# Three half-precision passes in place of float32 for the value and output weights of a head

## What is computed

```
wuk = w_uk.reshape(H, DN, KVL)
q_lat = jnp.einsum('bhsd,hdr->bhsr', q_nope, wuk)
scores = jnp.einsum('bhsr,btr->bhst', q_lat, c_kv) + jnp.einsum('bhsd,btd->bhst', q_rope, k_rope[:, 0])
...
out_lat = jnp.einsum('bhst,btr->bhsr', probs, c_kv)
wuv = w_uv.reshape(H, DV, KVL)
out = jnp.einsum('bhsr,hdr->bhsd', out_lat, wuv)
out = out.transpose(0, 2, 1, 3).reshape(b, s, H * DV)
return out @ w_out
```

## Time and profile before

| | |
|---|---|
| median of 3 runs | 2105.26 us (2104.92 to 2106.75) |
| profiled execution | 2106.01 us, its span 2104.2 us, clock 0.999 |
| PE busy | 2071.2 us, 98% of the span |
| DVE, ACT, POOL busy | 1274.1, 738.0, 364.9 us |
| chain that ended last | PE 96% |
| group 0's loop and the switch quad's slot 0 | about 177 to 885 us of the span |

### The profile page before, as it was taken

One profiled execution on the slowest core, in us unless ns is written; L12 is line 12 of the kernel. 1 busy time (PEld: TensorE's weight loads), 2 busy tenths in 40 slices (PEclk: granted clock), 3 DMA queues, 4 the chain that ended last, 5 costly groups with the idle time before them and its releaser, 6 DMA issues.

```text
span 2104.2 us, 29620 instructions
## 1 busy us (share of the span) xinstructions
PE 2071.2 (98%) x10688; PEld 1732.1 (82%) x10688; DVE 1274.1 (61%) x2114; ACT 738.0 (35%) x1931; POOL 364.9 (17%) x319
## 2 busy tenths in 40 slices
PE   6999999999999999999999999999999999999999
PEld 5787888888888888888888888888888768888887
DVE  4636666766666676666666666666667772333321
ACT  3324333333333333433333333333333555232221
POOL 2012212212121222121111212112121201000000
PEclk9999999999999999999999999999999999999999
DMA  5616343535353443557434244342435381202010
GB/s 212 240 62 222 105 173 103 193 115 188 115 205 121 158 135 142 201 192 265 135 115 144 70 150 134 106 154 70 150 117 198 114 313 53 81 1 81 1 41 40
DMA packets 63017, 284.78 MB, mean 135 GB/s; under 512 B 6640, under 2 KB 7280, under 8 KB 51440
## 3 DMA queue, kind: packets, MB, share of 16 engines
q1 hardware_dynamic: 62960, 284.00, 39.2%
HBM read 172.83 MB, written 111.15 MB: 135 GB/s over the span
## 4 chain that ended last, share of the span: by engine, by line
PE 96%; DVE 1%; DMA 1%; ACT 1%; POOL 0%; issue 0%; DVEq 0%; SPq 0%; ACTq 0%; POOLq 0%
PE at_out L53 11%; PE at_out L54 11%; PE at_out L55 11%; PE at_qbank L53 6%; PE at_qbank L55 6%; PE at_qbank L54 6%; PE at_qbank L946 6%; PE at_qbank L947 6%; PE at_score L738 4%; PE at_score L736 3%; PE at_turned L745 3%; PE at_qbank L692 2%; PE at_value L55 2%; PE at_value L54 2%; PE at_value L53 2%; PE at_score L737 1%
## 5 line engine op out<-in xcount | busy, mean ns | idle before, releaser
L1511 DVE TENSOR_TENSOR at_acc<-at_out,at_acc 128x512 f32<-128x512 f32 x512 | 352.1, 688 | 95.7 <-PE at_out L55 87.4
L53 PE MATMUL at_out<-at_wvo,at_val_hi 128*128 128x512 f32 x1024 | 402.5, 393 | 0.7 <-DVE at_acc L1511 0.7
L54 PE MATMUL at_out<-at_wvo,at_val_hi 128*128 128x512 f32 x1024 | 401.7, 392 | 0.0
L55 PE MATMUL at_out<-at_wvo,at_val_lo 128*128 128x512 f32 x1024 | 400.0, 391 | 0.0
L1059 ACT ACTIVATE at_probs<-at_probs,at_row_stats 128x128 f32<-128x128 f32 x512 | 199.8, 391 | 379.6 <-DVE at_row_stats L1489 379.6
L1276 POOL TENSOR_TENSOR at_probs<-at_probs,at_row_stats 128x512 f32<-128x512 f32 x128 | 133.3, 1041 | 819.1 <-DVE at_row_stats L1494 819.1
L55 PEld LDWEIGHTS at_out<-at_wvo,at_val_lo 128*128 128x128 f32 x1024 | 192.4, 188 | 42.7
L53 PEld LDWEIGHTS at_out<-at_wvo,at_val_hi 128*128 128x128 f32 x1024 | 193.3, 189 | 35.1 <-DVE at_acc L1511 1.8
L54 PEld LDWEIGHTS at_out<-at_wvo,at_val_hi 128*128 128x128 f32 x1024 | 193.0, 188 | 31.3
L1065 ACT ACTIVATE at_pT_hi<-at_turned 128x512 fp32r<-128x512 f32 x128 | 76.4, 597 | 318.6 <-PE at_turned L745 318.6
L738 PE MATMUL at_score<-at_tok,at_qrope 128*128 128x256 f32 x512 | 170.9, 334 | 0.0
(11 more groups left out here) (183 smaller groups left out, 4162.4 us busy)
## 6 DMA issues: line engine op xcount, KB each, us to landing
wvo_d<-at_wvo SPq DMA_DIRECT2D x16, 2048.0 KB, 7.4
parts_d<-at_rope_parts SPq DMA_DIRECT2D x32, 1024.0 KB, 7.0
at_qrope<-parts_d SPq DMA_DIRECT2D x128, 256.0 KB, 5.0
at_wvo<-wvo_d SPq DMA_DIRECT2D x16, 2048.0 KB, 8.5
ab_raw<-in_w_heads SPq DMA_DIRECT2D x32, 576.0 KB, 4.7
cr_ctx<-in_context SPq DMA_DIRECT2D x16, 1024.0 KB, 7.6
wabs_d<-at_wabs SPq DMA_DIRECT2D x16, 768.0 KB, 7.5
at_wabs<-wabs_d SPq DMA_DIRECT2D x16, 768.0 KB, 5.3
```

The source lines that it names most:

```text
L53: pe.matmul(out, w_hi, x_hi, start=first, stop=False)
L54: pe.matmul(out, w_hi, x_lo, start=False, stop=False)
L55: return pe.matmul(out, w_lo, x_hi, start=False, stop=last)
L1511: dve.tensor_tensor(at, outb[n][:], at, ALU.add).then_inc(added, 1)
```

## The change

In the 29 heads of the slots `absorb_head` gives way to `absorb_half`, called twice: half 0 between `values` and `output(s, 1)`, half 1 at the end of the slot. Each half is three float32r passes over 512 columns. The preparation and the opening keep `absorb_head`. The halves are cut so:

- ACT (`cut_half`): behind its `turn` it copies the head's 128 x 128 value weights to `ab_uv_hi` and the first 128 x 512 output weights to `ab_proj_hi`; behind its `values` it copies the other 128 x 512 into the same `ab_proj_hi`, once PE is through with half 0 (`ab_mm`). ACT, not PE, now waits for the ring's load.
- POOL (`cut_half`): as its first work in the slot it takes the low halves of the value weights and of the first output weights, in place in the ring; then, behind `rope_sums` if there is one but ahead of `normalise`, that of the second.
- PE waits for POOL's low half (`w_lo_done`) before each half.
- ACT's `take_head` waits in slots 5 and 7 for the end of `output(s, 1)`, since that reads the `wvo` buffer which it writes. DVE's order is unchanged.

```diff
+            def absorb_half(m, s, n, i, use, taken):
+
+                pe.wait_ge(w_lo_done, cuts(m, s, n))
+                pe.wait_ge(q_taken, taken)
+                low = ring_low[i]
+                three_passes(pe, qbank[use % 2][:], uv_hi[:], low[:, 0:DV], proj_hi[:],
+                             low[:, DV + n * CH:DV + (n + 1) * CH], True, True).then_inc(ab_mm, 1)
...
+                part = absorbed(kind, s)
+                if part and part[0] == "B":
+                    absorb_half(m, s, 0, (AHEAD + part[3]) % 2, use[s] + 1, first + use[s])
                 output(m, s, 1)
...
-                        absorb_head(i, bank_use, first + bank_use - 1)
+                        absorb_half(m, s, 1, i, bank_use + 1, first + bank_use)
...
+            def cut_half(n, i, part):
+
+                act.wait_ge(ab_mm, part + n)
+                if n == 0:
+                    act.activation(uv_hi[:], ring[i][:, 0:DV], ACT.Copy)
+                act.activation(proj_hi[:], ring[i][:, DV + n * CH:DV + (n + 1) * CH], ACT.Copy).then_inc(w_hi_done, 1)
...
+                if part and what == "B":
+                    act.wait_ge(ring_in[i], 16 * (ITEMS // 2 * m + (AHEAD + at) // 2 + 1))
+                    cut_half(0, i, count)
                 if s + 2 < end:
                     exps(m, s + 2)
...
+                if part and what == "B":
+                    cut_half(1, i, count)
...
+                        if place(s)[0] == h // 2:
+
+                            act.wait_ge(out_ready, 4 * (STEPS * m + s + 1))
                         take_head(h, use[s] + 1, count)
...
+            def cut_half(m, s, n, i):
+
+                pool.wait_ge(w_hi_done, cuts(m, s, n))
+                low = ring_low[i]
+                if n == 0:
+                    pool.tensor_tensor(low[:, 0:DV], ring[i][:, 0:DV], as_f32(uv_hi[:]), ALU.subtract)
+                cols = slice(DV + n * CH, DV + (n + 1) * CH)
+                pool.tensor_tensor(low[:, cols], ring[i][:, cols], as_f32(proj_hi[:]), ALU.subtract).then_inc(w_lo_done, 1)
...
+                if heads:
+                    cut_half(m, s, 0, (AHEAD + part[3]) % 2)
                 if finish:
                     rope_sums(first + USE[kind][s - 1] + 3)
+                if heads:
+                    cut_half(m, s, 1, (AHEAD + part[3]) % 2)
                 if s + 2 < end:
                     normalise(m, s + 2)
```

More of the change, by code:

```diff
@@ L144, in decoder @@
         ring = [home(200928 + 4 * ITEM_B * i, f"ab_raw{i}", [P, ITEM_B]) for i in range(2)]
+        uv_hi = at(TABLES + 2048, "ab_uv_hi", [P, DV], F32R)
+        proj_hi = home(198656, "ab_proj_hi", [P, CH], F32R)
+        ring_low = [home(200928 + 4 * ITEM_B * i, f"ab_low{i}", [P, ITEM_B], F32R) for i in range(2)]
         wvo, qlat, qrope = [wvo0, wvo1], [qlat0, qlat1], [qrope0, qrope1]
@@ L297, in decoder, with cuts @@
         AHEAD, ITEMS = 5, 6
+        CUT = {0: 0, 5: 1, 6: 2, 7: 3}
+        def cuts(m, s, n):
+            return len(PIECES) + 2 * (QUAD * m + CUT[s]) + n + 1
         x_chunks = x.rearrange("(c b p) d -> c p b d", c=CHUNKS, p=P)
@@ L855, in slot @@
                     rope(ROPE_AT[s], use[s] + 1, first + use[s])
[L856 removed]
+                if part:
                     what, _, _, at = part
                     i, bank_use = (AHEAD + at) % 2, use[s] + 1
[L859 removed]
                     if what == "A":
+                        pe.wait_ge(ring_in[i], 16 * (ITEMS // 2 * m + (AHEAD + at) // 2 + 1))
                         absorb_pair(i, bank_use, first + bank_use - 1)
                     else:
[L863 removed]
+                        absorb_half(m, s, 1, i, bank_use + 1, first + bank_use)
             def cross_turn(b):
@@ L1132, in slot @@
                     turn(m, s + 1)
+                part = absorbed(kind, s)
+                if part:
+                    what, h, ahead, at = part
+                    i, count = (AHEAD + at) % 2, 2 * (AHEAD + ITEMS * m + at)
+                if part and what == "B":
+                    act.wait_ge(ring_in[i], 16 * (ITEMS // 2 * m + (AHEAD + at) // 2 + 1))
+                    cut_half(0, i, count)
                 if s + 2 < end:
@@ L1145, in slot @@
                     act.activation(wqr[:, 0], wqr_raw, ACT.Copy).then_inc(wqr_hi, 1)
-                if part := absorbed(kind, s):
-                    what, h, ahead, at = part
-                    count = 2 * (AHEAD + ITEMS * m + at)
+                if part:
                     if what == "A":
@@ L1309, in slot @@
                 finish = s - 1 in ROPE_AT and end > STEPS
+                part = absorbed(kind, s)
+                heads = part is not None and part[0] == "B"
+                if heads:
+                    cut_half(m, s, 0, (AHEAD + part[3]) % 2)
                 if finish:
                     rope_sums(first + USE[kind][s - 1] + 3)
+                if heads:
+                    cut_half(m, s, 1, (AHEAD + part[3]) % 2)
                 if s + 2 < end:
```

## The result

| | before | changed |
|---|---|---|
| median of 6 runs each, us | 2105.09 | 2095.65 |
| lowest and highest | 2104.91, 2106.75 | 2094.69, 2097.34 |
| profiled execution | 2106.01 | 2096.1 |
| its span | 2104.2 | 2093.9 |

The changed kernel takes 0.9952 of the time before, with a 95% interval of 0.9942 to 0.9962: 9.4 us less. The forecast was 9.4 less, 2095.9. The passes that the title calls half-precision are the float32r passes over high and low halves.

What follows compares the result with a forecast made beforehand. PE, busy 98% at 2.4 GHz, was taken to bound the kernel. 28 heads at 0.357 us give 10.0, less 0.6 for stalls, 9.4 us: 2095.9 for the median; range 2093.5 to 2100.3.

Steps and rivals of the forecast that it cites:

- Removed and added, 0.36 a head: On PE, two float32 matmuls of 1.72 us give way to six float32r passes of 1.36: 0.36 us gained a head.
- Half 0 finds its operands: At half 0's start, ACT's copies and POOL's low halves are ready with over 2 us to spare; free.
- Half 1's chain: In slot 5, half 0's end, ACT copy, POOL subtraction, PE: operands ready 0.26 us early; then `normalise` delays the turn's load 0.10.
- The allowance of 0.02 a head: At the next slot's `turn`, behind `normalise`: 0.02 us lost a head with every link at its upper bound, 0.6 us in all.
- 28 heads, and nothing in quad 0: Quad 0's slot 0 gains nothing, as PE waits behind ACT for the rope weights' load; 28 heads left, 10.0 us.
- The clock's 1.7 us either way: Behind quad 0's wait, a lowered clock costs about 1.7 us; taken as unchanged, 1.7 either way for the range.
- Rival 4's second half: No slow clock behind quad 0's wait: 10.0 + 1.7 us gained, 2093.6; the whole rival has chance 0.04.
- The sum: Whole kernel: 10.0 - 0.6 = 9.4 us gained, 2095.9 for the median; chance 0.60.
- rival 1: Chain through `normalise` longer than its rows by 0.1 to 0.25 us: 0.05 to 0.2 a head, 2097.3 to 2101.0; chance 0.24.
- rival 3: POOL decides: PE waits each slot for `normalise` behind a subtraction of 1.85 us, not 1.29; slower, 2109.7; chance 0.03.
- Rivals 1 to 3: Chain through `normalise` too long, in three sizes; the middle one, 0.3 to 0.5 us more, gives 2102 to 2108, chance 0.09.
- The sign that the forecast named for them: In PE's list, the `turn` waiting for `at_probs` or half 1 for low halves, 0.1 us or more each slot.

Runs made afterwards that it cites:

- the repeat on one chip: The unmodified changed kernel measured again, beside the kernel before on the same chip: 2095.32 us, 0.9950 of before.
- the repeat with two subtractions: Changed kernel plus two 28-column POOL subtractions between second low half and `normalise`, run again on another chip: 2102.07 us, 0.9983 of before; first time 2101.66.

## Why the prediction was right, step by step

- **Removed and added, 0.36 a head: right in size, with luck in its parts.** The three passes of half 0 take 0.69 us and those of half 1 0.71 (352.39 to 353.10), where the rope's spacing gave 0.68 each. Why half 1's stand 0.237 apart stays open: it is so with and without `normalise` in the chain. Six passes are thus 1.40 and leave 0.32, not 0.36; the 0.04 at the start of the next slot, which I had not seen and which comes with the placing, makes it whole. Two small misses of opposite sign; the head's sum is 0.36 by the slots. The Trainium skill, FP8 and Floating Point Precision, section TensorE Precision Notes, counts true float32 as 4 passes; if every pass cost the same, three would gain 0.43 a head, an estimate. The trace doesn't agree with that gain: 1.40 us for six passes, where two float32 matmuls took 1.72, a fifth less. It doesn't refute the count of four: a quarter of one float32 matmul is 0.215 us, and a float32r pass, with a weight load of its own, took 0.227 to 0.237. The row of the pass itself was the better basis.
- **Half 0 finds its operands: right.** They are 3.6 us early, also in slot 5.
- **Half 1's chain: right to 0.04 at each point.** Counted from half 0's start, ACT's copy begins at +0.88 (forecast 0.88), POOL's subtraction at +1.60 (1.59), its end is at +2.89 (2.88), that of `normalise` at +3.89 (3.92), the turn's load at +3.94 (3.98), the turn at +4.15 (4.11 without stall). The copy took 0.64, not 0.60: my row was a copy from a PSUM bank, this one reads SBUF, which may be the reason. The 0.04 was made up by a shorter link from ACT to POOL, 0.08 where 0.11 was assumed, and by `normalise` starting 0.03 ahead of the subtraction's end. What I had no row for, POOL to PE, was 0.05.
- **The allowance of 0.02 a head: not needed, the one term of the sum that was wrong.** The load is 0.02 behind the pass ahead, forecast 0.10, and the cover for the turn is about 0.17, where I had read 0.15 from rows of another kind of matmul. So even the upper bound of 0.17 would have cost next to nothing, and the margin is 0.15 and not 0.05. Moving `normalise` out of the chain brought nothing. I had subtracted 0.6 us for it.
- **28 heads, and nothing in quad 0: right in size, the reason half right.** That PE's wait ends by the load's landing held: the copy began at 194.06 and 194.74 in the two profiles, and PE resumed 0.68 apart. Counted from the start of slot 0, the copy begins at 16.6 to 17.7 us in the ten traces, so this moves by a microsecond from one execution to the next. The 0.74 us of the difference between the traces come from there for the most part, and not from the change.
- **The clock's 1.7 us either way: a term that was mis-sized.** It is 0. I multiplied the missing clock by PE's time, though the earlier trace rows show DVE busy 2.93 of 3.00 us in that very stretch. Rival 4's second half falls with it.
- **The sum.** 10.0 less 0.6 was forecast. The 28 heads gave 10.1 by the slots and there was no stall, so the sum should have been 10.0. The medians differ by 9.4, but their interval, 8.0 to 12.2 us (0.4 to 0.6% of 2105), holds 10.0 as well, and the repeat on one chip gave 10.8. That the forecast met the median to a tenth is luck; its mechanism was right to 0.6. In rival 1 its prices don't quite follow from its terms: 0.05 to 0.2 a head on top of 2095.3 is 2096.7 to 2100.9, not 2097.3 to 2101.0, and rival 3's 4.2 us above 2105.3 is 2109.5.
- **Rivals 1 to 3** would have needed 0.1 us or more in the chain beyond its rows. The place is as they said, and beyond the cover so is the steepness: two small subtractions there cost 6.75 us, and 2.1 us of bare chain turns the change into a loss. But only ACT's copy was longer than its row, by 0.04. The sign that the forecast named for them, a wait for POOL of 0.1 us or more in PE's list, was a poor one: with two subtractions 0.25 a head is lost and PE's list shows nothing, while the weight loads' list does.

## What to carry to other kernels

Where a multiplication's operands are to be cut into halves by other engines, cost the passes from a pass of the same shape in the trace, and then follow the last operand's chain with all its links to the next thing that PE needs from that engine, not only to the pass itself. Put enough of PE's other work between the parts to cover the chain; here 2.76 us did, with 0.15 to spare, and with none between them the same instructions were 3.5% slower than the kernel before. Look for PE's short waits in the list of its weight loads too. Before pricing a slow clock or a wait, look which engine is busy all through the stretch behind it.

## What the runs showed of the hardware

- A float32r pass of 128 x 512 costs PE 0.227 to 0.237 us at the granted clock of 1.00, and a float32 matmul of that shape 0.86, which is 3.6 to 3.8 such passes.
- What a late weight load costs is its distance behind the start of the 512-column matmul ahead, less what is covered. For the turn's transposes about 0.17 us is covered (distance, lost: 0.02, 0; 0.14, at most 0.01; 0.19, 0.03; 0.21, 0.04; 0.29, 0.12; 0.30, 0.14; 0.43, 0.25), for a float32r pass 0.12 (0.15, 0.03; and 0.22, 0.10: in the kernel before, pass at 1641.08, load at 1641.30, the next two passes at 1641.31 and 1641.64). Beyond 0.23 the late matmul starts together with its load (350.26 and 350.26; 353.27 and 353.27).
- POOL's subtraction of 128 x 512 in place in the ring has a median of 1294 ns over 58, where one that writes elsewhere than it reads had 1292; one of 28 columns took 0.24 us, and two in a row started 0.20 apart, so back to back instructions on POOL overlap by 0.04.
- The slow clock behind PE's wait in quad 0 doesn't follow the wait's length alone. The clock over the three microseconds behind the wait was 1.00 behind 2.43 us in the changed kernel's profile and behind 2.18 in the repeat with two subtractions, but 0.53 behind 2.27 in the first run of that same kernel, 0.53 behind 2.55, 0.76 behind 2.85 and 0.50 behind 3.56. What decides it stays open.
